# Layers 0 and 1 of a four-layer graph network: score products graph by graph in column halves of TensorE, in place of 128x128 blocks

## The reference, cut to what matters

```python
# layer 0
q, k = split(h @ Wqk);  v = h @ Wv
agg = einsum('bij,bjd->bid', adj, k * mask)
w   = inv_scale * mask * einsum('bid,bid->bi', q, agg)
x   = x + softmax(w, axis=1)[:, :, None] * v
# layer 1
weight = einsum('bqd,bkd->bqk', query, keyt)       # query, keyt, value: h @ W.T + b
weight = adj * exp(weight)
weight = weight / sum(weight, axis=2)
x      = x + einsum('bqk,bkd->bqd', weight, value)
```

## Time and profile before

| | us |
|---|---|
| median of three runs | 2643.1 |
| profiled execution | 2638.46 |
| its span | 2636.7 |
| TensorE matmul busy | 2566.0 (97%) |
| VectorE busy | 1268.9 (48%) |
| GpSimd busy | 885.5 (34%) |
| ScalarE busy | 847.2 (32%) |

### The profile page before, as it was taken

One profiled execution on the slowest core, in us unless ns is written; L12 is line 12 of the kernel. 1 busy time (PEld: TensorE's weight loads), 2 busy tenths in 40 slices (PEclk: granted clock), 3 DMA queues, 4 the chain that ended last, 5 costly groups with the idle time before them and its releaser, 6 DMA issues.

```text
span 2636.7 us, 39165 instructions
## 1 busy us (share of the span) xinstructions
PE 2566.0 (97%) x16095; PEld 2126.6 (81%) x16095; DVE 1268.9 (48%) x2524; ACT 847.2 (32%) x1557; POOL 885.5 (34%) x1248
## 2 busy tenths in 40 slices
PE   9999999999999999999999999999979999999999
PEld 5788888888888878788888888888757878788887
DVE  2455455444445543443334433443546565656563
ACT  3333333333333324233333333333322222223231
POOL 3444444444444432342224322343332121212120
PEclk9999999999999999999999999999989999999999
DMA  4011111111111122121111111111212121212110
GB/s 140 21 37 37 37 55 53 37 37 37 37 37 37 37 80 73 28 72 38 37 37 49 61 37 37 38 58 60 101 44 68 35 68 35 68 35 68 35 53 32
DMA packets 103922, 130.75 MB, mean 50 GB/s; under 512 B 46576, under 2 KB 46656, under 8 KB 103744
## 3 DMA queue, kind: packets, MB, share of 16 engines
q1 hardware_dynamic: 103744, 128.25, 14.4%
HBM read 77.90 MB, written 50.33 MB: 49 GB/s over the span
## 4 chain that ended last, share of the span: by engine, by line
PE 82%; POOL 6%; DVE 6%; issue 3%; ACT 2%; DMA 1%; SPq 0%; POOLq 0%; ACTq 0%; DVEq 0%
PE bank L305 37%; PE bank L295 26%; PE bank L320 4%; PE bank L285 3%; PE bank L609 3%; POOL stA L1233 2%; PE bank L500 2%; PE bank L371 2%; POOL stA L1231 2%; PE bank L528 1%; DVE yt L941 1%; PE bank L274 1%; PE bank L511 1%; DVE rst L912 1%; DVE yt L956 1%
## 5 line engine op out<-in xcount | busy, mean ns | idle before, releaser
L305 PE MATMUL bank<-w_hi,h3T_hi 128*128 128x512 f32 x768 | 305.9, 398 | 18.5 <-DVE Z_lo L641 18.5
L305 PE MATMUL bank<-w_lo,h3T_hi 128*128 128x512 f32 x768 | 300.1, 391 | 0.0
L305 PE MATMUL bank<-w_hi,h3T_lo 128*128 128x512 f32 x768 | 300.1, 391 | 0.0
L1308 POOL TENSOR_TENSOR zt<-zt,sm 128x512 f32<-128x512 f32 x64 | 66.2, 1044 | 544.4 <-DVE sm L830 544.4
L981 ACT ACTIVATE hn<-x,stA 128x512 f32<-128x512 f32 x192 | 151.5, 812 | 261.1 <-POOL stA L1233 261.1
L305 PEld LDWEIGHTS bank<-w_hi,h3T_hi 128*128 128x128 f32 x768 | 144.8, 189 | 51.2 <-DVE Z_lo L641 21.8
L305 PEld LDWEIGHTS bank<-w_hi,h3T_lo 128*128 128x128 f32 x768 | 144.6, 188 | 30.6
L305 PEld LDWEIGHTS bank<-w_lo,h3T_hi 128*128 128x128 f32 x768 | 144.7, 188 | 29.3
L1281 POOL TENSOR_TENSOR vv_lo<-vf,vv_hi 128x512 fp32r<-128x512 f32 x64 | 82.3, 1285 | 227.1 <-ACT vv_hi L967 227.1
L641 DVE TENSOR_TENSOR cT_lo<-bank,cT_hi 128x256 fp32r<-128x256 f32 x128 | 45.4, 417 | 225.6 <-ACT cT_hi L967 225.6
L641 DVE TENSOR_TENSOR Z_lo<-bank,Z_hi 128x512 fp32r<-128x512 f32 x128 | 84.2, 687 | 143.1 <-ACT Z_hi L967 143.0
(11 more groups left out here) (248 smaller groups left out, 6674.0 us busy)
## 6 DMA issues: line engine op xcount, KB each, us to landing
mid<-x SPq DMA_DIRECT2D x32, 1024.0 KB, 4.6
x<-mid SPq DMA_DIRECT2D x32, 1024.0 KB, 5.7
x<-in_x SPq DMA_DIRECT2D x16, 1024.0 KB, 5.5
out<-x SPq DMA_DIRECT2D x16, 1024.0 KB, 4.5
abf<-in_adj SPq DMA_DIRECT2D x64, 64.0 KB, 4.5
adj<-in_adj SPq DMA_DIRECT2D x128, 32.0 KB, 3.0
w_raw<-in_L_gnn_Wk SPq DMA_DIRECT2D x3, 1024.0 KB, 11.4
wqk<-in_L_gnn_Wqk SPq DMA_DIRECT2D x2, 1024.0 KB, 6.3
```

The costliest lines, as they stand in the source:

```text
L305: ins = eng.matmul(b[:], h[l][:, k, ts], W[r][:, k, :], start=(k == 0 and i == 0), stop=(last and k == 3 and i == 2))
```

## The change

`scores` now takes the two graphs of a block one at a time. For each block t and each k it issues two matmuls: graph 0 writes partitions 0 to 63 and graph 1 writes partitions 64 to 127, each with a 128-deep, 64-wide stationary operand and 64 moving columns. They alternate between the two column halves of the array. The result of block t goes to columns 64t to 64t+63, so that the useful scores lie in the first 256 columns of the bank with nothing between them. The 16 matmuls of a call become 32 smaller ones. VectorE's two instructions at L746 become one over 128 partitions, and ScalarE's eight exponentials become four over 128 partitions; the counts that other engines wait for are halved to match.

```diff
@@ scores (TensorE)
                 for t in range(4):
-                    ts = slice(t * 128, (t + 1) * 128)
                     for k in range(4):
-                        ins = eng.matmul(b[:, ts], left[:, k, ts], right[:, k, ts], start=(k == 0), stop=(k == 3))
+                        for i, h in enumerate(HALF):
+                            ts = slice(t * 128 + i * 64, t * 128 + i * 64 + 64)
+                            ins = eng.matmul(b[h, t * 64:(t + 1) * 64], left[:, k, ts], right[:, k, ts], start=(k == 0), stop=(k == 3))
                 ins.then_inc(full, 1)
@@ TensorE's loop
-                    scores(("s0", g), gT[0], hF[0], (v_am, 2 * g + 2))
+                    scores(("s0", g), gT[0], hF[0], (v_am, g + 1))
...
-                    scores(("s1", g - 1), gT[1], hF[1], (a_ex, 8 * g))
+                    scores(("s1", g - 1), gT[1], hF[1], (a_ex, 4 * g))
@@ VectorE
-                dve.wait_ge(a_ex, 8 * (g - 1))
+                dve.wait_ge(a_ex, 4 * (g - 1))
...
-                    bv = t4(bank.of(("s0", g))[:])
-                    for h in HALF:
-                        eng.tensor_tensor(am[h, :, :], bv[h, :, h], am[h, :, :], ALU.mult).then_inc(v_am, 1)
-                    dve.wait_ge(v_am, 2 * g + 2)
+                    eng.tensor_tensor(am[:], t4(bank.of(("s0", g))[:, 0:256]), am[:], ALU.mult).then_inc(v_am, 1)
+                    dve.wait_ge(v_am, g + 1)
@@ ScalarE
                     for t in range(4):
-                        for h in HALF:
-                            eng.activation(ex[h, t, :], bv[h, t * 128 + h.start:t * 128 + h.stop], ACT.Exp,
-                                           bias=ecol[(g - 1) % 2][h, 4 + t:5 + t]).then_inc(a_ex, 1)
+                        eng.activation(ex[:, t, :], bv[:, t * 64:(t + 1) * 64], ACT.Exp,
+                                       bias=ecol[(g - 1) % 2][:, 4 + t:5 + t]).then_inc(a_ex, 1)
@@ GpSimd
-                    pool.wait_ge(a_ex, 8 * g)
+                    pool.wait_ge(a_ex, 4 * g)
```

## The result

The changed kernel takes 2584.7 us (median of four runs, 2584.2 to 2585.8) against 2643.4 us (four runs, 2640.5 to 2643.8): a ratio of 0.978, 95% interval 0.976 to 0.980. The two profiled executions, 2638.46 and 2584.85 us, differ by 53.6 us. All lines of `kernel.py` behind the change have moved by one or two: L320 is L321 now, L360 is L361, L641 is L642, L1088 is L1086.

What follows compares the result with a forecast made beforehand. TensorE's list alone was taken to set the time. Savings of 45.8 (scores) + 1.3 (exponentials) = 47.1 us gave 2591.5 us for the profiled execution and, with the 4.6 us median offset, 2596 us; range 2588 to 2608 us.

Steps and rivals of the forecast that it cites:

- a cover that was none: In each loop step, v0 products were said to hide the chain from layer 1 scores to plo, by some 0.2 us.
- the readers of the scores: ScalarE's exponentials after layer 1 scores: 2.64 us to become 1.3, worth nothing in the loop; VectorE's single multiply also nothing.
- an offset carried over: Median of runs stood 4.6 us above the profiled execution; this was added to 2591.5 us, giving 2596 us.
- s0, 16 calls: Layer 0 score products on TensorE: each call from 4.04 to 2.67 us, 1.37 us saved 16 times, 21.9 us.
- s1, 15 calls and the last: Layer 1 score products on TensorE: 1.5 us saved 15 times, 22.5 us, plus 1.4 us for the last call.
- last group's open wait: At the last group no v0 products hide TensorE's 3.7 us wait for plo; shorter exponentials take 1.3 us off.
- The reading of L528: Layer 2's four-quadrant matmuls, 64 records in 1.09 us, taken to show column halves fed from the same partitions work together.
- the short entry behind L351: Small transpose before layer 1 scores starts 0.15 us ahead of them; if that stays, 1.55 us saved a call, otherwise 1.38.
- Turns: Rival: the column halves take turns in the score calls, 1.84 us more a call, about 2654 us, slower; chance 7%.
- partial overlap: Rival: column halves overlap in part in the score calls, a pair taking about 85 ns, about 2624 us; chance 5%.
- series: Rival: loads and matmuls of both halves run one after another in the score calls, 2772 us; chance 1%.
- new wait: Rival: with shorter loop steps hnB or plo comes late, one microsecond in 15 steps, about 2611 us; chance 4%.

Runs made afterwards that it cites:

- s0 alone: Kernel before with only the layer 0 scores in column halves and VectorE's one multiply; layer 1 scores and eight exponentials as before: 2616.5 us, ratio 0.991.
- four exponentials alone: Kernel before with its old score blocks but four exponentials of 128 partitions, part of layer 1 computed from wrong scores: 2635.8 us, ratio 0.998.

## Why the prediction fell short

The direction and the mechanism of the score products were right; the time came out below the range. Three steps failed: a cover that was none, the price of the readers of the scores with the clock behind them, and an offset carried over. The table takes apart the 53.6 us between the two profiled executions, and the 5 us more between the medians:

| term | forecast | measured |
|---|---|---|
| s0, 16 calls | 21.9 | 16 x 1.36 = 21.8 |
| s1, 15 calls and the last | 23.9 | 15 x 1.55 + 1.4 = 24.7 |
| plo late in every step | 0 | 15 x 0.18 = 2.7 |
| last group's open wait | 1.3 | 3.67 - 1.82 = 1.85 |
| the low clock behind it | 0 | 3.4 us fewer, 1.7 |
| step 0, wait for the softmax row | 0 | 1.55 - 1.14 = 0.4 |
| median less profiled execution | 0 | about 5 |

The terms of the traces add up to 53.2 us, and all lie in layers 0 and 1. That this is so near 53.6 is in part luck. Followed by the same instructions, the changed kernel's execution is 0.9 us behind at its start (the first matmul of L274 at 13.11 us for 12.26), 51.6 us ahead in layer 2 (a piece of L528, now L529, at 1216.88 us for 1268.47), and gains 2.0 us more from there to the end, where the code is the same. Two traces of the kernel before drift apart by 1.3 us over that part. The wait in step 0 is TensorE's for the softmax row behind s0; it shrank with VectorE's one multiply for two, which takes 0.42 us for 0.88 there. It is 1.1 us wherever that was in (also with s0 alone) and 1.6 us where it was not (also with four exponentials alone).

*The score products.* Column halves fed from the same 128 partitions work side by side, at the rate taken from L500: 1.86 us from the first start to the last in both. The reading of L528, that a row half serves both column halves at once, was the step that carried the forecast, and it held. The rule of the Trainium skill that loads overlap only across row groups ("TensorE: Matmul & The Clock Gate", "The mechanism") isn't borne out here: 64 loads and matmuls, all of one row group, go in 2.02 us. The same section also lets a load go ahead into a background weight buffer; no run here tells whether that is what happens. For s1 the short entry behind L351 stayed, so 1.55 and not 1.5.

*The cover that was none.* "That cover is thin, some 0.2 us" is the first step that failed. I set the end of `plo`, 490.66, against the start of the sums' piece in the chain, 490.86. But pieces there begin where the piece before ends, and a matmul's record ends well after the next could start. The start of the first sum, 490.80, 0.33 us behind the last wide start where 0.23 is the rule, would have shown it as late. Four exponentials alone show that 0.18 us a step was lost, 2.7 us in all, which the sum put at nothing.

*The readers of the scores.* Each exponential lasts as long as before (315 ns against 308), as taken. But the four start 0.20 us apart where the eight started 0.33 us apart, so 1.7 us went and not 1.3. In the last group the open wait falls by 1.85 us, these 1.7 and 0.15 of the dearer way out of s1, which TensorE now spends before the wait, and the shorter stretch at the lower clock behind it gives 1.7 us more: 3.5 us for the 1.3 forecast. The clock stands nowhere in the sum; at most it is part of the 3 us that the range gave to the places between layers. The parts of that range, 2, 1, 3, 2 and 4 us, add up to 12 us, which would have reached down to 2584; the stated bottom was 2588.

*The offset.* "The median of the runs stands 4.6 us above that execution", carried over to the changed kernel as it stood, is the step that cost most. The execution profiled was one of the quick ones. Part of the offset is a stretch at the 1.2 GHz level at 68 us which comes in some executions and not in others (2.5 to 2.8 us in two traces), another part the longer wait for `cT_lo` (some 1.5 us). Eight runs of the changed kernel lie within 2584.2 and 2586.7 us. Why they rarely or never have the stretch is open, and so is what else makes up a run of 2643.5 us; no trace of such a run was caught.

None of the rivals came about. Turns, partial overlap and series are ruled out by the 2.02 us; no new wait appeared from 100 to 940 us. Without alternation a call would have been between the forecast and the partial overlap.

## What to carry over

Where two independent small products share the contraction rows, put them in the two column halves and let them alternate: with fp32 operands 64 columns wide it took 3.57 us down to 2.02, less 0.2 us for each way in and out, so such calls are worth putting side by side. Judge whether a chain is covered by the distance between starts on the engine that waits, not by where pieces of the chain begin. And before a sum worked out from one execution is moved to a median, ask whether that execution is one of the quick ones: here that was 5 of 59 us.

## What the runs showed of the hardware that I had not expected

- ScalarE: 64x64 exponentials on alternating partition halves start 333 ns apart and last 308; 128x64 ones last 315 and start about 200 ns apart. The bigger ones follow each other faster.
- TensorE's order: 64 records in two column halves take 32 rounds of 57.5 ns where the half changes every 2 records, 33 where it changes every 4, 43 where it changes every 8. By the starts of the last case the other half runs up to three records ahead of its turn.
- The clock fell to the 1.2 GHz level behind an idle time of 1.1 or 1.6 us in some executions and stayed at 2.4 GHz behind the same idle time in others. One trace gives no certain price for it.
